# Small matrix products of blocks 0 and 2 padded to the full 128 rows and columns

## What is computed

```python
# block 0: NL = 6 layers, 16 heads of 8 features
for i in range(6):
    xn = adaln(x, cond, n1_w[i], n1_b[i])
    q, k, v = split(xn @ qkv_w[i].T)
    x = x + attn(rope(q), rope(k), v, src_mask) @ so_w[i].T          # 56 x 56 keys
    xn = adaln(x, cond, n2_w[i], n2_b[i])
    q = rope(xn @ cq_w[i].T)
    k, v = rope(context @ ck_w[i].T), context @ cv_w[i].T
    x = x + attn(q, k, v, ctx_mask) @ co_w[i].T                      # 56 x 1500 keys
    xn = adaln(x, cond, n3_w[i], n3_b[i])
    x = x + gelu(xn @ f1_w[i].T + f1_b[i]) @ f2_w[i].T + f2_b[i]
# block 2: 16 heads of 64; the keys are the 1500 context rows and the 56 latents
kv_in = concat(layer_norm(context), lat)
x = x + softmax(q k^T / 8) v @ Wo.T
```

## Time and profile before

| | |
|---|---|
| median of 3 runs | 6659.54 us (6654.61 to 6660.7) |
| span of the profiled execution | 6652.9 us |
| TensorE (PE) busy | 6159.3 us, 93% |
| weight loads (PEld) busy | 4429.8 us, 67% |
| VectorE busy | 3930.9 us, 59% |
| ScalarE busy | 3325.9 us, 50% |
| GpSimd busy | 2242.2 us, 34% |
| mean granted TensorE clock | 0.946 of full speed |

### The profile page before, as it was taken

How to read it: one execution, slowest core, us unless ns; L and a number is a source line. 1 busy time by engine, 2 the same in 40 slices (tenths; PEclk the granted TensorE clock), 3 DMA queues, 4 the chain that set the end, 5 groups by cost and what they waited for, 6 DMA issues and landing times.

```text
span 6652.9 us, 141291 instructions
## 1 busy us (share of the span) xinstructions
PE 6159.3 (93%) x56229; PEld 4429.8 (67%) x56229; DVE 3930.9 (59%) x8713; ACT 3325.9 (50%) x6401; POOL 2242.2 (34%) x2179
## 2 busy tenths in 40 slices
PE   6899899999999989999989999999789999989998
PEld 4566566665666656666653877777567777756983
DVE  3777777777777777777765334444544444444553
ACT  1565656656566565665654334444333333333763
POOL 4554555555555555555520000000011111136440
PEclk6899999999999999999989889999789999998998
DMA  1665656656666565665740010000000000021000
GB/s 56 105 111 83 99 94 99 106 91 103 93 98 111 85 100 100 96 108 87 110 95 5 13 38 29 29 33 24 26 15 15 10 15 12 13 81 36 2 1 23
DMA packets 396488, 407.90 MB, mean 61 GB/s; under 512 B 125575, under 2 KB 372946, under 8 KB 393786
## 3 DMA queue, kind: packets, MB, share of 16 engines
q1 hardware_dynamic: 395834, 398.85, 33.8%
HBM read 158.00 MB, written 0.46 MB: 24 GB/s over the span
## 4 chain that ended last, share of the span: by engine, by line
PE 69%; DVE 8%; POOL 7%; issue 6%; ACT 4%; DMA 2%; SPq 1%; POOLq 1%; DVEq 0%; ACTq 0%
PE psum L2214 10%; PE psum L2181 9%; PE psum L1551 6%; PE psum L1539 6%; PE psum L1525 6%; PE psum L2226 4%; PE psum L1565 4%; PE psum L1573 3%; PE psum L1671 3%; POOL slot_context L3399 2%; PE psum L434 2%; DVE row_max L1890 2%; PE psum L420 2%; PE psum L1680 1%; DMA key_stack<-key_parts 1%
## 5 line engine op out<-in xcount | busy, mean ns | idle before, releaser
L1890 DVE TENSOR_REDUCE row_max<-psum 112x1 f32<-112x500 f32 x2304 | 1443.7, 669 | 285.3 <-PE psum L1539 280.3
L2011 ACT ACTIVATE weights<-psum 125x448 f32<-125x448 f32 x2304 | 1155.4, 544 | 769.3 <-PE psum L1525 754.3
L1525 PEld LDWEIGHTS psum<-query_stack,key_stack 121*125 121x125 bf16 x9216 | 830.4, 140 | 368.4 <-issue 165.5
L1539 PE MATMUL psum<-key_stack,query_stack 97*112 97x500 bf16 x2304 | 907.8, 395 | 102.1 <-DVE row_max L1890 78.9
L1525 PE MATMUL psum<-query_stack,key_stack 121*125 121x112 bf16 x9216 | 932.3, 224 | 70.1 <-ACT weights L2011 65.0
L2767 POOL TENSOR_TENSOR l_ctx_v<-l_ctx_v,l_ctx_w 125x512 f32<-125x512 f32 x48 | 61.1, 1272 | 2223.1 <-DVE l_ctx_v L2761 2223.1
L2294 DVE TENSOR_REDUCE l_stat<-psum 128x1 f32<-128x1500 f32 (+1 forms) x224 | 391.6, 1748 | 576.6 <-PE psum L2181 576.6
L2214 PE MATMUL psum<-l_ctx_v,l_turned 125*128 125x128 f32 x5376 | 713.6, 281 | 16.0 <-ACT l_turned L2252 12.3
L2214 PEld LDWEIGHTS psum<-l_ctx_v,l_turned 125*128 125x128 f32 x5376 | 643.0, 191 | 58.5 <-ACT l_turned L2252 39.9
L1551 PE MATMUL psum<-weights,values 125*17 125x112 f32 x18432 | 678.0, 266 | 0.2 <-ACT weights L2011 0.2
L1551 PEld LDWEIGHTS psum<-weights,values 125*17 125x17 f32 x18432 | 379.4, 97 | 263.6 <-ACT weights L2011 144.7
(11 more groups left out here) (527 smaller groups left out, 10264.3 us busy)
## 6 DMA issues: line engine op xcount, KB each, us to landing
key_stack<-key_parts SPq DMA_DIRECT2D x1728, 125.0 KB, 4.5
ctx_t<-in_ctxT SPq DMA_DIRECT2D x96, 750.0 KB
l_ctx_v<-in_ctxV SPq DMA_DIRECT2D x32, 750.0 KB
query_stack<-query_parts SPq DMA_DIRECT2D x576, 28.0 KB, 3.7
l_ctx_t<-in_ctxT SPq DMA_DIRECT2D x16, 750.0 KB
slot_context<-in_ctxV SPq DMA_DIRECT2D x16, 750.0 KB
key_stack<-ctx_mask_rows SPq DMA_DIRECT2D x576, 3.9 KB
sm_w<-in_sm_w SPq DMA_DIRECT2D x3, 2048.0 KB
```

Source lines behind the costliest of these rows:

```text
L1525: mm = e.matmul(self.k.psum[0:KN, h, (p % 4) * QC:(p % 4 + 1) * QC], ks[:, p, kt * KN:(kt + 1) * KN], q[:, p * QC:(p + 1) * QC])
L1539: e.matmul(self.k.psum[0:QC, 2 + n % 2, 0:500], q[0:ROWS_MAX, p * QC:(p + 1) * QC], ks[0:ROWS_MAX, p, c * 500:(c + 1) * 500]).then_inc(sel ...
L1890: e.tensor_reduce(self.largest[:, i % PAIRS, i // PAIRS:i // PAIRS + 1], k.psum[0:QC, 2 + i % 2, 0:500], AX.X, ALU.max, negate=True).then_ ...
L2011: e.activation(half(self.p[kt % 2], h), self.k.psum[0:KN, h, 0:HALF], ACT.Exp).then_inc(self.exped.sem, 1)
```

## The change

Seven kinds of small products get operands of full size, and the tiles they read are widened and filled with zeros once:

- `rows`: 25 columns become 128. `flip` and `sflip`: 56 rows become 128, and the moving identity grows from 56 to 128 columns.
- `turn`, `sturn`, `st`: 56 columns become 128; the pieces overlap, the rows beyond 56 of the result are not read.
- the mask product: 1 row becomes 128, of which 127 are zero.
- block 2's own-key tile: 56 columns become 125 when turned, and 56 rows become 125 when multiplied; the copy of the last group takes 125 partitions.

The number of instructions on TensorE stays the same. VectorE gets eight more memsets and a drain at the start of block 0 and three memsets at the start of block 2; GpSimd gets one memset and a drain at the start of block 0.

```diff
+TURN_COLS, SELF_COLS = 3 * S + 128, (R - 1) * S + 128
...
-            self.src_mask = sb("src_mask", [1, T], BF16)[:, :]
-            self.one_row = sb("one_row", [1, 128], BF16)[:, :]
+            self.src_mask = sb("src_mask", [128, T], BF16)[:, :]
+            self.one_row = sb("one_row", [128, 128], BF16)[:, :]
...
-                tr = e.transpose(side.bank(*key)[0:S, i * 128:(i + 1) * 128], self.acc[:, i * S:(i + 1) * S],
+                tr = e.transpose(side.bank(*key)[:, i * 128:(i + 1) * 128], self.acc[:, i * S:i * S + 128],
                                  k.ident[:, :])
...
-            e.transpose(side.bank(*key)[:, 0:S], self.o, k.ident[0:S, 0:S]).then_inc(side.filled, 1)
+            e.transpose(side.bank(*key)[:, 0:128], self.o, k.ident[:, :]).then_inc(side.filled, 1)
...
-            e.transpose(side.bank(*key)[0:1 + 3 * PAIRS, 0:QC // 2].bitcast(BF16), self.m_part,
+            e.transpose(side.bank(*key)[:, 0:QC // 2].bitcast(BF16), self.m_part,
...
                 e.matmul(bk[:, 0:R * S].rearrange("p (r s) -> p r s", r=R), self.one_row,
-                         of_batch(self.src_mask, b).unsqueeze(1).broadcast_to([1, R, S]), start=True, stop=False,
+                         of_batch(self.src_mask, b).unsqueeze(1).broadcast_to([128, R, S]), start=True, stop=False,
...
-                        tr = e.transpose(side.bank(*key)[0:S, (r - lo) * 128:(r - lo + 1) * 128], self.sp[i % 2][:, r, :],
-                                         k.ident[:, :])
+                        tr = e.transpose(side.bank(*key)[:, (r - lo) * 128:(r - lo + 1) * 128],
+                                         self.sp_cols[i % 2][:, r * S:r * S + 128], k.ident[:, :])
...
-                e.transpose(side.bank(*key)[:, 0:S], self.so, k.ident[0:S, 0:S]).then_inc(side.filled, 1)
+                e.transpose(side.bank(*key)[:, 0:128], self.so, k.ident[:, :]).then_inc(side.filled, 1)
...
-        e.memset(self.one_row, 1.0)
+        e.memset(self.one_row, 0.0)
+        e.memset(self.m_part, 0.0)
+        for a in (self.acc[:, 2 * QC:], self.sacc[:, 2 * QC:], self.o, self.so, *(a[:, R * S:] for a in self.sp_cols)):
+            e.memset(a, 0.0)
+        e.drain()
+        e.memset(self.one_row[0:1, :], 1.0)
...
     def gpsimd(self, e):
         side = self.side
+        e.memset(self.src_mask, 0.0)
+        e.drain()
...
-                    mm = e.matmul(k.psum[:, 6, 0:128], pt[0:S, t, :], self.own_values(b), start=False, stop=True)
+                    mm = e.matmul(k.psum[:, 6, 0:128], pt[:, t, :], self.own_values(b), start=False, stop=True)
...
-                tr = e.transpose(bk[0:rows, t * 128:(t + 1) * 128], self.p[j % 2][:, c0:c0 + rows], k.ident[:, :])
+                tr = e.transpose(bk[0:KN, t * 128:(t + 1) * 128], self.p[j % 2][:, c0:c0 + KN], k.ident[:, :])
...
-            self.lat = sb("l2_latents", [S, B, 128])[:, :, :]
+            self.lat = sb("l2_latents", [KN, B, 128])[:, :, :]
...
         e.tensor_scalar(self.cond1, k.cond, 1.0, None, ALU.add)
+        e.memset(self.lat, 0.0)
+        for p in self.cross.p:
+            e.memset(p[:, self.cross.width:], 0.0)
         ln_vector(e, k, LN_IN2, k.x, k.xn)
```

More of the change, by code:

```diff
@@ L1267, in __init__ @@
             self.neg = sb("neg_max", [QC, PAIRS])[:, :]
-            self.m_part = sb("neg_max_parts", [QC, 1 + 3 * PAIRS], BF16)[:, :]
-            self.acc = sb("sums", [128, 2 * QC])[:, :]
+            self.m_part = sb("neg_max_parts", [QC, 128], BF16)[:, :]
+            self.acc = sb("sums", [128, TURN_COLS])[:, :]
             self.inv = sb("inverse_sum", [S, 16])[:, :]
-            self.o = sb("heads_out", [S, 128])[:, :]
+            self.o = sb("heads_out", [128, 128])[:, :]
             self.att = sb("attended", [128, QC])[:, :]
             self.qd = sb("l0_qd", [128, 2, T])
-            self.sp = [sb(f"self_p{i}", [128, R, S])[:, :, :] for i in range(2)]
+            self.sp_cols = [sb(f"self_p{i}", [128, SELF_COLS])[:, :] for i in range(2)]
+            self.sp = [a[:, 0:R * S].rearrange("p (r s) -> p r s", r=R) for a in self.sp_cols]
             self.spt = [sb(f"self_pt{i}", [S, H * S])[:, :] for i in range(2)]
@@ L1699, in phase_tensor @@
                 for m in range(4):
-                    tr = e.transpose(side.bank(*key)[0:S, m * 128:(m + 1) * 128], self.sacc[:, m * S:(m + 1) * S],
+                    tr = e.transpose(side.bank(*key)[:, m * 128:(m + 1) * 128], self.sacc[:, m * S:m * S + 128],
                                      k.ident[:, :])
@@ L1735, in max_parts_vector @@
     def max_parts_vector(self, e, s):
-        neg, m = self.neg, self.m_part[:, 1:].rearrange("q (p j) -> q p j", j=3)
+        neg, m = self.neg, self.m_part[:, 1:1 + 3 * PAIRS].rearrange("q (p j) -> q p j", j=3)
         e.wait_ge(self.max_read.sem, self.max_read(s, 3 * PAIRS - 1))
@@ L1993, in phase_scalar @@
                     e.wait_ge(side.filled, side.at("sturn", ph, i - 1))
-                e.activation(self.sacc, side.bank(*key)[:, 0:2 * QC], ACT.Copy).then_inc(side.emptied(*key), 1)
+                e.activation(self.sacc[:, 0:2 * QC], side.bank(*key)[:, 0:2 * QC], ACT.Copy).then_inc(side.emptied(*key), 1)
             if t == a + 5:
@@ L2120, in __init__ @@
         sb = lambda *a: k.sb(st, *a)
-        self.p = [sb(f"{name}_weights{i}", [128, self.width])[:, :] for i in range(2)]
+        self.p = [sb(f"{name}_weights{i}", [128, self.tiles * KN])[:, :] for i in range(2)]
         self.pt = [sb(f"{name}_turned{i}", [KN, self.tiles, 128])[:, :, :] for i in range(2)]
@@ L2220, in weigh_tensor @@
         for g, (lo, m) in enumerate(self.groups):
-            rows = KN if lo < KT else S
             bk = turn.bank("p", j, g)
@@ L2248, in weights_out @@
         e.wait_ge(turn.filled, turn.at("p", j, g))
-        o = self.pt[j % 2][0:rows, lo:lo + m, :]
-        i = turn.bank("p", j, g)[0:rows, 0:m * 128].rearrange("p (k r) -> p k r", k=m)
+        o = self.pt[j % 2][:, lo:lo + m, :]
+        i = turn.bank("p", j, g)[0:KN, 0:m * 128].rearrange("p (k r) -> p k r", k=m)
         if g < 2:
@@ L2276, in attend_scalar @@
                 stat = self.stat[i % 4]
-                e.activation(self.p[i % 2].rearrange("p (c n) -> p c n", c=self.n_s),
+                e.activation(self.p[i % 2][:, 0:self.width].rearrange("p (c n) -> p c n", c=self.n_s),
                              k.psum[:, 0:self.n_s, 0:self.step], ACT.Exp, bias=stat[:, 1:2],
```

12 lines of the change are left out of this document (6 added, 6 removed).

## The result

| | before | after |
|---|---|---|
| median of 4 runs | 6660.1 us | 6558.9 us (6555.0 to 6561.1) |
| span of the profiled execution | 6652.9 us | 6553.2 us |
| mean granted clock, profiled execution | 0.946 | 0.953 |

The changed kernel takes 0.9844 of the time before, interval 0.983 to 0.9858: 101 us less.

A forecast was written before the change was run, and what follows sets the result against it. TensorE, 69% of the chain, was taken as the bound. Block 0's 38.4 us plus block 2's 31.4 less 2.4 for added work gave 67.4 off 6652.9, so 6585.5; with 6.6 added, 6592 us, range 6572 to 6618.

The forecast's parts named there:

- the price of a border: On TensorE, each border between a full product and a small one was said to cost 0.09 to 0.10 us.
- own-key product: Block 2: padding was to save 0.28 us at each of 112 places, 31.4 us, all reaching the end.
- mask product: Block 0: padding was to save 0.15 us at each of 96 places on the chain, 14.4 us.
- both flips: Block 0: `sflip` was to save 79 x 0.14 = 11.1 us and `flip` 73 x 0.08 = 5.8 us.
- `rows`: Block 0: padding was to save 0.17 us at each of 42 places on the chain, 7.1 us.
- wide transposes: `turn`, `sturn` and `st`, 1440 in all: same pace at 56 and 125 columns, so 0 gained or lost.
- how block 0 handed on: Block 0: 290 of 384 padded pieces counted on the chain, so 38.4 us of the 51.8 freed reach the end.
- The base: Whole kernel: the median of the runs was taken as 6.6 us above the profiled span of 6652.9 us.
- rival 1: The 1440 padded transposes are paced by their wider weight loads: 94 us lost on the chain, 6686 us; chance 0.04.
- Block 0 giving nothing back (2): Block 0's savings end in waits, leaving 29 us gained: 6631 us; chance 0.10.
- Everything coming through (3): All time freed on TensorE in both blocks reaches the end, 80.8 us: 6579 us; chance 0.20.
- That the change does not do what it says (4): TensorE's stops belong to neighbouring products and bank waits, so only the memsets' cost is left: 6662 us; chance 0.03.

The follow-up runs named there:

- e1: Kernel before with only block 2's own-key tile padded, block 0 as before: 6621.5 us, ratio 0.9944.
- e7: Kernel before with only block 2's own-key tile changed, to 65 rows and columns: 6621.3 us, ratio 0.9934.
- e11: Kernel before with the mask product padded to 128 rows and issued three times: 6620.3 us, ratio 0.9941.
- e12: The changed kernel measured once more, with no further edit: 6568.0 us, ratio 0.9863 to the kernel before.
- e15: Kernel before with the one-row mask product issued twice: 6679.2 us, ratio 1.003.
- e10: Kernel before with the mask product left out, so the source mask's bias is missing from the scores: 6600.1 us, ratio 0.991.
- e3: Kernel before with only the mask product of the self attention padded to 128 rows: 6608.8 us, ratio 0.9925.
- e16: Kernel before with only the mask product padded, to 64 rows instead of 128: 6663.6 us, ratio 1.0008.
- e4: Kernel before with only the turned maxima (`rows`) widened to 128 columns: 6656.5 us, ratio 0.9995.
- e6: Kernel before with only block 2's own-key tile changed, to 64 rows and columns: 6661.2 us, ratio 0.9994.

## Why the prediction was wrong

**The mechanism was right, but not complete.** Borders between small and full products cost TensorE time, padding takes them away, the transposes of 56 columns have none, and block 2 hands nearly all of it on.

**First step that failed: the price of a border.** "So each border between a full product and one with at most 56 rows, or with 25 columns, costs 0.09 to 0.10 us" counts the wait up to the next start. Behind the small product there is a second piece: the first full product behind a border holds TensorE 0.10 us longer, and the load of the weights for the one after it starts 0.10 us later too, as the views of PEld show. It showed in block 2 as 431 ns against 331, behind the mask product as 153 against 49, and before bfloat16 products as 99 to 100 against 53 to 55. The rows of before had it, one product further on than I read. The terms and what they measured:

| term | predicted | measured |
|---|---|---|
| own-key product | 112 x 0.28 = 31.4 us | 0.385 an item, 43 direct; 37 (e1) and 45 (e7) timed, 39 at the full clock |
| mask product | 96 x 0.15 = 14.4 | 25 direct, 50 timed, 19 to 20 at the full clock |
| both flips | 11.1 + 5.8 = 16.9 | 16 direct, 29 timed, 5 to 6 at the full clock |
| `rows` | 42 x 0.17 = 7.1 | 20 direct, 2 or none timed, none at the full clock |
| wide transposes | 0 | 5 lost directly, 8 to 11 at the full clock |
| memsets | -2.4 | -1.2 in block 2; 0.9 of VectorE's time in block 0, its effect on the end not shown |
| granted clock | not counted | 0.947 to 0.952, at most 31 us |

The flips' direct sum came out right by two errors: the flip behind the 17-column products takes 0.165 us and not 0.11, and what follows both gained the 0.05 that I had not counted.

**Second step: the clock.** The sum took the granted clock of before as given, so it had no term for it. What 0.001 of mean clock goes with in time: about 2.6 us among the 49 runs of the kernel before (0.943 to 0.949), 4.9 among the five runs of kernel e1 (6652.8 us at 0.941, 6618.4 at 0.948), 4.2 in kernel e11, which gains 44 us for 0.0105. At most it can be 6.7: 0.001 is 13.3 us at the lower level, each losing at most half. For the whole change, 0.005 at 2.6 to 4.9 us for each 0.001 is 13 to 25 us, an estimate; it fits into the 31 us that the changed kernel gains where one of the traces is at the lower level. With the 68 us at the full clock and some 5 that the padded products gain at the lower level (7% of 68), the estimate makes 86 to 98, against 101 measured. For kernel e12, the changed kernel again, 68 us come at the full clock too, and its clock is 0.0015 higher than before: 77 to 80, against 90. So the sum comes out low both times, by 3 us or more and by about 10, and that rest is not explained. By the Trainium skill ("TensorE: Matmul & The Clock Gate", section "What's actually happening") the lower level is the default and activity releases the throttle. The order of the clocks in kernels e15, e10, e3 and e11 agrees in direction. But kernel e7 widened 224 products of block 2, freed 40 us and has 0.946, so width alone is not enough.

Why the clock rose stays open. In block 0 of the kernel before, from 250 us on, TensorE sits idle 34 times for 2.3 to 2.6 us, and 22 of the 33 falls of the clock come shortly behind one of these waits. Kernel e16 has 34 such waits and 34 falls, kernel e11 34 waits and only 23 falls. Wider products may let the clock come through such a wait, or the edits may only have moved the waits in time; kernels e4, e6, e15 and e16 move them too and stay at 0.947 to 0.948, which speaks against the second, but no run separates the two.

**Third step: how block 0 handed on.** The count of padded pieces on the chain, 290 of 384, made 38.4 us of 51.8. The gaps freed 25 + 16 + 20 us less the 5 of the wide transposes, 56 in all, and 29 arrive at the full clock (31, an estimate, with the 6% of the products left out), little more than half and not three quarters. The largest loss is 9 us of longer gaps before the row-maxima products (line 1539), which wait for VectorE there. So block 0 was counted 8 us too high (37.1 with its memsets) and block 2 about 9 too low (30.3), and the forecast of 67.4 meets the 68 us at the full clock by luck. What is missing in the end is the 31 us at the lower level.

**The base was not at fault.** I put 6.6 us between the profiled span and the time. The runs show 1.7 to 1.9 between each execution's time and its span; the profiled one was simply about 5 us faster than the median. As the forecast was for the median, adding the 6.6 was right, and the 33 us missed all lie in the gain.

**The rivals.** Wide loads in the open (rival 1) exist, but only behind the 17-column products, at 0.033 us each, far below the 0.06 that I gave as the point where they decide. Block 0 giving nothing back (2) is right for `rows`, and for two thirds of what the flips freed. Everything coming through (3) was nearest, for another reason than the one given. That the change does not do what it says (4) fell with kernels e6 and e7.

## What to carry to other kernels

Measure a change of array form over three products, not one: the wait before the small product, its own follower, and the gap inside the next group, which together are 0.30 us for the mask product here and 0.385 for the two instructions of the own-key product. Rows of zeros that bring the product to 65 rows are enough to end it, and products of one small form put side by side pay it once. Count what of it arrives for each kind of product, as `rows` and the flips gave little or nothing at the full clock and the mask product nearly all. Where the granted clock is below 1 in several stretches, give it its own term in the sum and compare it over several runs before reading a gain of one per cent as freed time.

## What had not been expected of the hardware

- The limit lies between 64 and 65 rows of the stationary operand: 0.62 us against 0.34 from product to scores, 6661.2 against 6621.3 us.
- A border makes the follower's own successor late too: 431 against 331 ns in float32, 100 against 53 to 55 in bfloat16.
- Behind the 17-column products the width of the next load shows: the first gap is 132 ns with 56 columns and 165 with 128; in the middle of a run of products both are 109.
- Three padded products in place of one small one added about 7 us of work and made the kernel 37.5 us faster, at a clock of 0.9575 instead of 0.947.
- As many waits of 2.3 to 2.6 us in block 0, 34, go with 33 falls of the clock in the kernel before and with 23 in kernel e11.
